# One kernel of attention and experts on one Trainium2 core: the next chunk's statistics, projections and rope placed five half-steps later

## What is computed

```
x = x + attention(layernorm(x))      # 16 heads of 16, q and k rotated (rope), softmax, output projection
x = x + experts(layernorm(x))        # RMS norm, gate, top 2 of 8 experts
# inside attention
q = rope(x @ Wq.T + bq); k = rope(x @ Wk.T + bk); v = x @ Wv.T + bv
out = softmax(q k^T / 4) v @ Wo.T + bo
# inside experts: p1 = nf @ w1[e] + b1[e]; g, lin = clipped halves of p1
act = g * sigmoid(1.702 g) * (lin + 1); p2 = act @ w2[e] + b2[e]; out = xc + sum_e combine[e] * p2[e]
```

## Time and profile before

| | us |
|---|---|
| median of 3 runs | 1222.55 (1220.27 to 1226.99) |
| the profiled execution, whole | 1218.1 |
| its span, first to last instruction | 1216.3 |
| PE busy | 974.2 (80%) |
| DVE busy | 861.2 (71%) |
| ACT busy | 699.3 (57%) |
| POOL busy | 400.5 (33%) |

### The profile page before, as it was taken

One profiled execution on the slowest core, in us unless ns is written; L12 is line 12 of the kernel. 1 busy time (PEld: TensorE's weight loads), 2 busy tenths in 40 slices (PEclk: granted clock), 3 DMA queues, 4 the chain that ended last, 5 costly groups with the idle time before them and its releaser, 6 DMA issues.

```text
span 1216.3 us, 17776 instructions
## 1 busy us (share of the span) xinstructions
PE 974.2 (80%) x5241; PEld 414.5 (34%) x5313; DVE 861.2 (71%) x1702; ACT 699.3 (57%) x905; POOL 400.5 (33%) x344
## 2 busy tenths in 40 slices
PE   4719897879678997898578898887878999996575
PEld 2402222234232443333233343323333444344243
DVE  5723204768658896786586899586966997898797
ACT  2318895746458574764447675664657776771232
POOL 2413304422244334433135334441321333233243
PEclk9759998989899999988799998998989999997686
DMA  4253342303424241333403334241323442411010
GB/s 148 81 111 59 90 90 63 91 27 79 102 53 105 65 100 58 84 82 76 105 26 84 79 91 101 53 109 44 91 67 77 99 105 58 99 41 39 31 52 31
DMA packets 56443, 92.72 MB, mean 76 GB/s; under 512 B 7162, under 2 KB 41346, under 8 KB 53250
## 3 DMA queue, kind: packets, MB, share of 16 engines
q1 hardware_dynamic: 37892, 66.14, 24.0%
q10 hardware_dynamic: 18432, 25.17, 7.1%
HBM read 74.24 MB, written 17.04 MB: 75 GB/s over the span
## 4 chain that ended last, share of the span: by engine, by line
PE 47%; DVE 28%; issue 12%; ACT 4%; DMA 3%; POOL 2%; SPq 2%; another core or an unknown queue 1%; DVEq 0%; ACTq 0%; POOLq 0%
PE OP L644 12%; PE S L630 11%; PE D L616 7%; DVE th_sb L1052 3%; PE A L599 3%; PE D L543 3%; PE BB L599 3%; DVE act_sb L1057 3%; DVE g_sb L1035 3%; PE D L526 2%; DVE acc L1047 2%; DVE l_sb L1037 2%; ACT probs L761 2%; DMA X<-in_x 2%; DVE xn L895 2%
## 5 line engine op out<-in xcount | busy, mean ns | idle before, releaser
L761 ACT ACTIVATE probs<-S 128x1024 f32<-128x1024 f32 x512 | 511.9, 1022 | 245.9 <-PE S L630 239.5
L630 PE MATMUL S<-Qs,Ks 98*128 98x512 bf16 x1024 | 311.9, 397 | 66.1 <-issue 28.5
L644 PE MATMUL OP<-probs,V 128*17 128x512 f32 x2048 | 280.6, 621 | 2.7 <-ACT O L770 2.7
L848 POOL TENSOR_TENSOR act_lo<-act_sb,act_hi 128x512 fp32r<-128x512 f32 x128 | 165.0, 1289 | 224.9 <-DVE act_hi L1063 164.6
L616 PE MATMUL D<-W,act_hi 128*128 128x256 f32 x448 | 138.3, 338 | 40.9 <-DVE Vn L935 20.0
L630 PEld LDWEIGHTS S<-Qs,Ks 98*128 98x128 bf16 x1024 | 80.2, 100 | 252.9 <-issue 95.6
L1047 DVE SCALAR_TENSOR_TENSOR acc<-D,combh,acc 128x256 f32<-128x256 f32 x224 | 97.3, 476 | 79.7 <-PE D L616 79.6
L616 PE MATMUL D<-W,act_lo 128*128 128x256 f32 x448 | 119.0, 295 | 0.0
L842 POOL TENSOR_SCALAR W<-W2b 128x512 fp32r<-128x512 bf16 x64 | 44.2, 690 | 225.7 <-PE D L616 220.8
L737 ACT ACTIVATE th_sb<-g_sb 128x512 f32<-128x512 f32 x128 | 80.1, 626 | 64.0 <-DVE g_sb L1035 63.2
L1052 DVE SCALAR_TENSOR_TENSOR th_sb<-th_sb,g_sb 128x512 f32<-128x512 f32 x128 | 116.3, 909 | 0.1
(11 more groups left out here) (138 smaller groups left out, 1063.4 us busy)
## 6 DMA issues: line engine op xcount, KB each, us to landing
W<-in_w ACTq DMA_DIRECT2D x64, 256.0 KB, 2.7
Ks<-k_scr SPq DMA_DIRECT2D x32, 384.0 KB
W2b<-in_w ACTq DMA_DIRECT2D x64, 128.0 KB, 2.7
Ks<-k_scr SPq DMA_DIRECT2D x32, 256.0 KB
q_scr<-parts SPq DMA_DIRECT2D x16, 384.0 KB, 2.8
k_scr<-parts SPq DMA_DIRECT2D x16, 384.0 KB, 2.5
Qs<-q_scr SPq DMA_DIRECT2D x32, 192.0 KB
X<-in_x SPq DMA_DIRECT2D x8, 512.0 KB, 7.6
```

Of the source, the lines that this page charges most:

```text
L630: last = mm(S[:, j2, C * i:C * (i + 1)], Ks[0:SROWS + MROWS, g % 2, j, P * kt:P * (kt + 1)], Qs[0:SROWS + MROWS, g % 2, j, :], start=True, ...
L644: last = mm(OP[32 * j:32 * j + VW, :], V[:, kt, HG * g + j, :], probs[:, s % 2, C * j:C * (j + 1)], start=kt == 0, stop=kt == KT - 1)
L761: nc.scalar.activation(probs[:, s % 2, 2 * C * j2:2 * C * (j2 + 1)], S[:, j2, :], ACT.Exp, scale=SCALE).then_inc(exp_done, 1)
L848: tt(act_lo[:, e % 2, it, :], act_sb[:, a % 2, :], act_hi[:, e % 2, it, :].bitcast(FP32), ALU.subtract).then_inc(lo_s, 1)
```

## The change

Eleven entries of `AT` grow by five half-steps: `stats1`, `rstd1`, `xn`, `xT0`, `xT1`, `qk0` to `qk3`, `v0`, `v1`. The entries `rope`, `part1`, `length`, `part2`, `part3` and `guard`, `flag` are offsets from the `qk` entries, so those stages move along. `x_in` stays at half-step 0. The guard of the odd chunks goes from half-step 36 to 41, the flag from 44 to 49, the last `part3` from 40 to 45. Post-processing and experts stay where they are. The order of the first two chunks' preparation (`HEAD`) doesn't change. In `normalise`, DVE now waits for `half_s`, the mark of its own multiplication (L1093) of the group before, ahead of the transpose that overwrites what that multiplication read.

```diff
-    AT = {"x_in": 0, "stats1": 1, "rstd1": 1, "xn": 4, "xT0": 7, "xT1": 8, "qk0": 10, "qk1": 12, "qk2": 22,
-          "qk3": 30, "rope": 2, "part1": 3, "length": 5, "part2": 7, "part3": 10, "v0": 37, "v1": 42, "guard":
+    AT = {"x_in": 0, "stats1": 6, "rstd1": 6, "xn": 9, "xT0": 12, "xT1": 13, "qk0": 15, "qk1": 17, "qk2": 27,
+          "qk3": 35, "rope": 2, "part1": 3, "length": 5, "part2": 7, "part3": 10, "v0": 42, "v1": 47, "guard":
           1, "flag": 8, "x1_in": 0, "x1_b": 7, "wo0": 13, "wo1": 14, "stats2": 15, "rstd2": 16, "xc": 17, "ss":
...
                 dve.wait_ge(o_ev, G + 1)
+                if looped(G) or G:
+                    dve.wait_ge(half_s, G)
                 v.transpose(OT[:, :, :].rearrange("p k c -> p (k c)"), O[:, g % 2, :]).then_inc(ot_s, 1)
```

## The result

| | before | after |
|---|---|---|
| median, us | 1221.41 (1218.87 to 1226.99, 4 runs) | 1328.71 (1324.8 to 1330.85, 4 runs) |
| ratio | | 1.0868, 95% interval 1.0822 to 1.0914 |
| profiled execution, span | 1218.1, 1216.3 | 1329.0, 1327.2 |
| mean granted clock of TensorE | 0.908 | 0.861 |

The kernel became 107 us slower where 26 were forecast. The sign was right; the size was off by a factor of four.

A forecast was written before the change was run, and what follows sets the result against it. No engine fills the span; what counts is how far work pushes the 512 exponentials apart. -5.1 - 0.5 + 4 + 2.5 + 5 + 20.4 = +26.3 us on median 1222.55 gave 1249 us, range 1224 to 1273 us.

The forecast's parts named there:

- the term for tiles 2 and 3, lengths and v: Chunks 1 to 5, later stages moved into the experts: +1 us per chunk, between -1.5 and +4, +5 in all.
- The term for tiles 0 and 1: Chunks 1 to 5, from the output projection to `nfT`: +0.5 us per chunk, between -1 and +3, +2.5 in all.
- each shifted rope stalls ACT: Rival: every `part1` waits 2 to 4 us; upper bounds +68, half the excess gives +47, 1270 us; chance 0.15.
- The first half-steps: First 13 half-steps of chunks 2 to 5: +1 us per chunk, between -1.5 and +3, +4 in all.
- Chunk 1's load: Load of x ahead of chunk 1's first transpose: of PE's 6.38 us wait, 5.1 go, so -5.1 us.
- Chunk 0: First chunk: -0.5 us for the load of x, between -1.5 and 0; 0 for tiles 2 and 3.
- The guard: Chunks 1, 3, 5: `down` 2 waits longer for POOL's `lo` 3; 6.8 us each, between 4 and 9, +20.4 in all.
- The wait for `half_s`: DVE's new wait in `normalise`: costs nothing, its mark being set eight steps, over 16 us, earlier on the same engine.
- The flag and SP's queue: Odd chunks: next batch's q and k loads wait for the flag at 49, not 44; costs nothing, PE needs them later.
- hidden preparation: Rival: slack of half-steps 7 to 13 hides the preparation, -5 us in each of four chunks; about 1213 us, chance 0.09.
- cancelling terms: Rival: the preparation hides in slack but the guard costs its full +20.4, sum about +2; 1225 us, chance 0.14.
- the change does what it says: Rival claimed the opposite: DVE still waits for x at half-step 6 in chunks 2 to 5; 1255 us, chance 0.02.

The follow-up runs named there:

- the longer rope: `part1`, `length`, `part2`, `part3` two half-steps later: on the changed kernel 1279.63 us, on the kernel before 1239.14 us.

## Why the forecast was wrong

**The step that failed** is the pricing of the moved ropes, above all the term for tiles 2 and 3, lengths and v: "+1 us per chunk", +5 in the sum. Measured by single moves, tile 2 costs 38 us, tile 3 without the guard's reduction 38 and v 7: some 84 in place of 5. In the changed kernel itself the stretch from half-step 27 on, less the guard, is (92.4 - 17.7) / 5 = +14.9 a chunk, of which tile 2's own work, moved in from the row above, is 2.8 (the row above fell by 13.9 us in five chunks when tile 2 alone moved). The term for tiles 0 and 1, +2.5, measured some 14 (52 - 38, the difference of two runs). I had described both mechanisms in the text: tile 1's shuffle behind `ms`, tile 2's behind the gate's chain, "POOL, and the exponentials wait behind it". But I priced them by the nearest dense row, 1.93 us, and set half of that against hoped-for gains. That row belongs to a tile whose shuffle had no wait ahead of it. The price could have been read from rows: shuffle to `part1` takes 3.5 us (394.25 - 390.76 above; 3.6 in the kernel before, 380.89 - 377.29), and the shuffle could not start before DVE's last operation of the queue ahead. The rival "each shifted rope stalls ACT" was the true one. Its own bound, 2 to 4 us per `part1`, nearly holds (4.48 at tile 1, 3.62 at tiles 2 and 3, nothing at tile 0), but I cut it in half for the sum, and it counts one stall per tile where there are two more: the length product on PE, which holds the scores, and the `nsq` behind the experts on DVE, which holds the bank (4.34 us ahead of a `down` at half-step 40). The upper bound of that rival was +68, still short.

**What the sum left out** is the clock; it had a word of it in the guard's bounds only. PE stood at the lower level for some 145 us more than before. Half-steps 33 to 35 of chunks 2 and 3 show the price with the same matmuls in both: 6.15 us for 12.8 us more at the lower level (2 x 0.44 x 16.17 - 2 x 0.07 x 10.02), 0.48 us for each. By that rate the 145 us cost at most some 70, an estimate and an upper bound, since PE is not what the exponentials wait for at every moment. Against chunk 3, chunks 2 and 4 lose 12 us of it in half-steps 33 to 35 alone. These microseconds are inside the prices of the single moves above. How a move's price divides into waits and clock stays open.

**The first half-steps** came out as forecast, in size. The +1 a chunk was net of the two q tiles, which the prediction took out of this stretch at 5.9 us and put behind the output projection: that is why it has the output projection of chunk 3 "about 34" us after the chunk's start, and it began at 34.8 (525.47 - 490.68; 38.0 before). In the table chunks 2 to 5 fell by 3.2 to 5.2. Moving tiles 0 to 2 alone, without the statistics, gave -4.8 to -6.4 up to half-step 14, so statistics, `xn` and transposes cost 0.4 to 2.5 us a chunk, inside my -1.5 to +3. (Executions with an unmoved front differ by up to 3.4 us in a chunk there, so this is no sharp test.) How it came about was not all foreseen: the stall where `xn` stood in front of `g_sb`, 8.86 us in half-step 6, went; a new one of 7.28 came at half-step 10, which had cost 4.75, and 1.44 with the q tiles gone.

**Chunk 1's load**: -5.1 forecast, -5.3 measured up to half-step 14, but 1.9 of that came with tiles 0 to 2 alone. PE's wait at the transpose fell by 4.35 us to 2.03, 1.3 forecast. **Chunk 0**, where tiles 2 and 3 were to cost nothing, lost 2.1 us, and 1.5 more lie ahead of its first exponential; with the longer rope both were gone (-0.5). Why is open.

**The guard**: +20.4 forecast, 17.7 by the two kernels without the reduction, 6.8 and 5.9 per odd chunk. This working held, from POOL's return to the 10 us of PE: `down` 2 started 16.0 us after the maximum (620.37 - 604.41), 15.2 forecast. **The wait for `half_s`**: nothing, as forecast. **The flag and SP's queue**: PE's only wait for a load of q is 22.0 us, once, in both traces.

**The rivals that fell**: hidden preparation and cancelling terms (the 21.5 us of the first row are mostly the q tiles' work, which comes back in the second); the change does what it says. Even chunks longer by 2 to 3 was wrong, chunks 2 and 4 took 23 to 24 more; the text named the sign of it, "if ACT's waits at `part1` grow to many us".

## What to carry to other kernels

When a stage made of several engines is moved in a hand-made order, look at each of its instructions for what now stands directly ahead of it on its engine, and take the whole remaining wait, not half, whenever an engine on the backbone waits in order behind the last of them, and once for each engine that does. A schedule that was thinned in one place is thick in another: the same two half-steps of distance gave 49 us back in one kernel and cost 18 in the other. When you compare a forecast with a table by stretches, first say which work crosses a line of the table. And price each move by itself first: here the prices of the moves added up to within 12 us (53 + 59 + 7 against 107).

## What the runs showed of the chip

- The same 44 matmuls, PE busy without a gap, took 16.17 us at a granted clock of 0.56 and 10.02 us at 0.93 in two chunks of one execution; four matmuls that take 1.98 us otherwise took 3.78. The mean granted clock fell from 0.908 to 0.861 with a kernel that does the same work and waits more.
- DVE beside POOL: 1.64 us in place of 0.69 for an addition, 5.48 in place of 1.6 for `xn`, whose quarters end 0.15 us after the POOL instruction that they meet.
- One reduction over partitions (0.37 us of work) keeps POOL away for 13.3 to 13.9 us (551.32 - 538.05, 618.28 - 604.41) and costs the kernel before 25.7 us in four uses (1218.44 - 1192.71); nothing else that was tried won more than 3 us over it.
